# One block of the first MLP product moved across a chunk boundary on TensorE, and two bias sums held back in the tail

## What is computed

```
n  = layernorm(x)                                   # no gain or bias
h  = layernorm(n) * ln1_g + ln1_b
q, k, v = h@wq, h@wk, h@wv                           # 16 heads of 16
phi = elu(.) + 1
num = phi(q) @ (sum over the sequence of phi(k)^T v)
den = phi(q) . (sum over the sequence of phi(k))
y2 = n + (num / den) @ wo                            # 256 x 256
g  = layernorm(y2) * ln2_g + ln2_b
t  = gelu at the grid point nearest to g@w1          # steps of 0.1, w1 256 x 1024
xp = x + (y2 + t @ w2)                               # w2 1024 x 256
out = xp + (layernorm(xp) @ CB^T) * SCB/127 + bias   # CB 256 x 256
```

## Time and profile before

| what | value |
| --- | --- |
| median of 3 runs | 593.51 us |
| the profiled execution | 594.68 us, its span 592.9 us |
| mean granted TensorE clock | 0.981 of full speed |
| TensorE matrix multiplications | 549.6 us busy, 93% |
| VectorE | 466.2 us, 79% |
| ScalarE | 384.8 us, 65% |
| GpSimd | 338.8 us, 57% |

### The profile page before, as it was taken

The page is one execution under the profiler, slowest core; times in us unless marked ns, Lnnn a source line. Parts: engine busy times, 40 slices in busy tenths (PEclk is TensorE's granted clock), DMA queues, the critical chain, the costliest instruction groups (busy, mean ns, idle before and its releaser), DMA issues.

```text
span 592.9 us, 11272 instructions
## 1 busy us (share of the span) xinstructions
PE 549.6 (93%) x3610; PEld 490.9 (83%) x3610; DVE 466.2 (79%) x1067; ACT 384.8 (65%) x636; POOL 338.8 (57%) x328
## 2 busy tenths in 40 slices
PE   6899999999996889999999999999999999999893
PEld 6778788888885879889898898988988889898783
DVE  5889998688775487978879788788887888878645
ACT  2475664465565667858669586696865968758650
POOL 3431333324131367786776868768687676776662
PEclk9699998999999999999999999999999999999998
DMA  8321221121001010101101101011010110200001
GB/s 269 122 71 48 94 71 37 35 72 35 16 22 56 1 37 1 71 35 35 71 0 71 39 33 71 0 71 54 16 71 0 71 68 2 71 4 33 36 21 54
DMA packets 11419, 29.47 MB, mean 50 GB/s; under 512 B 2048, under 2 KB 4864, under 8 KB 11392
## 3 DMA queue, kind: packets, MB, share of 16 engines
q1 hardware_dynamic: 9472, 28.32, 13.4%
q10 hardware_dynamic: 1920, 0.79, 0.7%
HBM read 20.71 MB, written 8.39 MB: 49 GB/s over the span
## 4 chain that ended last, share of the span: by engine, by line
DVE 28%; PE 23%; issue 18%; ACT 15%; POOL 13%; DMA 2%; POOLq 1%; ACTq 0%; DVEq 0%; SPq 0%
PE psum L1002 22%; POOL f32r_arena L378 7%; DVE bn_stats L657 4%; ACT grid_index L580 3%; POOL f_arena L371 3%; DVE f_arena L793 3%; DVE f32r_arena L814 3%; ACT f32r_arena L593 3%; DVE f_arena L824 2%; DMA f_arena<-in_L_attn_x_dram 2%; DVE f32r_arena L810 2%; DVE bn_stats_b L657 2%; ACT f_arena L591 2%; ACT f32r_arena L528 2%; DVE f32r_arena L802 2%
## 5 line engine op out<-in xcount | busy, mean ns | idle before, releaser
L1002 PE MATMUL psum<-w_hi,f32r_arena 128*128 128x256 f32 x1280 | 176.9, 284 | 12.3 <-POOL f32r_arena L378 8.6
L1002 PEld LDWEIGHTS psum<-w_hi,f32r_arena 128*128 128x128 f32 x1280 | 164.0, 189 | 22.9 <-issue 16.9
L1002 PE MATMUL psum<-f32r_arena,w_hi 128*128 128x512 f32 x512 | 139.9, 403 | 1.5 <-issue 1.0
L378 POOL TENSOR_TENSOR f32r_arena<-f_arena,f32r_arena 128x512 fp32r<-128x512 f32 x64 | 85.9, 1342 | 94.6 <-ACT f32r_arena L593 54.1
L580 ACT ACTIVATE grid_index<-psum,w_bias_in_steps 128x512 int8<-128x512 f32 x128 | 86.7, 677 | 64.2 <-PE psum L1002 64.2
L1002 PEld LDWEIGHTS psum<-f32r_arena,w_hi 128*128 128x128 f32 x512 | 88.0, 188 | 19.9 <-ACT grid_index L580 5.8
L591 ACT ACTIVATE f_arena<-grid_index 128x512 f32<-128x512 int8 x128 | 80.9, 632 | 24.6 <-POOL f32r_arena L378 14.3
L593 ACT ACTIVATE f32r_arena<-grid_index 128x512 fp32r<-128x512 int8 x128 | 79.3, 619 | 0.0
L1002 PE MATMUL psum<-f32r_arena 128*128 128x256 f32 (+1 forms) x384 | 71.6, 336 | 2.0 <-DVE f32r_arena L696 2.0
L1002 PEld LDWEIGHTS psum<-f32r_arena 128*128 128x128 f32 x384 | 59.2, 195 | 8.4 <-issue 2.2
L802 DVE TENSOR_TENSOR f32r_arena<-f_arena,f32r_arena 128x512 fp32r<-128x512 f32 x64 | 63.2, 988 | 2.1 <-ACT f32r_arena L593 1.8
(11 more groups left out here) (116 smaller groups left out, 916.2 us busy)
## 6 DMA issues: line engine op xcount, KB each, us to landing
f_arena<-in_L_attn_x_dram SPq DMA_DIRECT2D x32, 512.0 KB, 3.3
out_dram<-f_arena SPq DMA_DIRECT2D x15, 512.0 KB, 2.7
f_arena<-in_L_attn_w_dram SPq DMA_DIRECT2D x2, 1024.0 KB, 12.6
out_dram<-f_arena SPq DMA_DIRECT2D x2, 256.0 KB, 3.3
phi_q<-in_L_attn_wk_dram ACTq DMA_DIRECT2D x1, 256.0 KB, 4.7
phi_q<-in_L_attn_wq_dram SPq DMA_DIRECT2D x1, 256.0 KB, 4.9
phi_q<-in_L_ffn_CB_dram SPq DMA_DIRECT2D x1, 256.0 KB, 7.0
phi_q<-in_L_attn_wo_dram SPq DMA_DIRECT2D x1, 256.0 KB, 7.5
```

Of the source, the lines that this page charges most:

```text
L378: nc.gpsimd.tensor_tensor(t_lo[m % SLOTS], tf[m % 2], t_hi[m % SLOTS].bitcast(F32), ALU.subtract).then_inc(s["t_lo_p"], 1)
L1002: return nc.tensor.matmul(out_, lhs, rhs, start=start, stop=stop, skip_group_check=True)
```

## The change

TensorE takes `up(i + 1, 0)` before `down(i, 7)` instead of behind it; the very first `up(0, 0)` stays where it was. GpSimd waits, ahead of its two sums in the tail, until both halves are normalised. No operation is added or taken away, apart from that wait. A line that is only "..." marks what is left out.

```diff
@@ the tail of GpSimd's program
             g.wait_ge(stored, CHUNKS * 16)
+            g.wait_ge(s["n_half"], 2)
             for h in range(2):
                 nc.gpsimd.tensor_tensor(half_tm(xb, h).rearrange("p (j d) -> p j d", j=TT // 2),
...
@@ TensorE, phase 2
                 def body(i, prv, main, nxt, attend_seq, attended):
                     if main:
-                        up(i, 0)
                         up(i, 1)
...
                     down(i, 6)
                     if attend_seq is not None:
                         attention(i + 2, attend_seq, 1)
+                    if nxt:
+                        up(i + 1, 0)
                     down(i, 7)
 
+                up(0, 0)
                 body(0, False, True, True, 0, 0)
```

## The result

The changed kernel takes 595.1 us (median of 12 runs) where the one before takes 592.8 in the same sessions: a ratio of 1.004, interval 1.002 to 1.0059, so about 2.4 us slower. I had predicted 1.2 us slower, inside a range of 591.0 to 598.4. The profiled execution has a span of 593.6 us, 0.7 us longer than that of before.

The account below looks back on a forecast made before the run. It took each chunk as bound by VectorE's chain from `down` 7 to `attention_out` plus TensorE's stretch after it. Boundaries + 3.5 and tail - 2.3 made + 1.2 us on 593.5, so 594.7 us, range 591.0 to 598.4.

Parts of the forecast that it names:

- The joint: `down` 7 at a chunk boundary: from it to `attention_out` the time is VectorE's, 7.09 us; the rest is TensorE's.
- the slack: Free time ahead of `down` 7, counted between starts: 0.71 us, where the moved block needs 0.94 us.
- The size at the boundaries: Cost of the moved block at 13 chunk boundaries: + 3.5 us in all, bounded by 0 and + 7.7 us.
- the bracket: Listed wait of TensorE ahead of `down` 7, counted from the modelled end of the last multiplication: 0.46 us.
- the 0.23 us of the working: At a chunk boundary `down` 7 ends this much later, and the delay passes on to `attention_out`.
- The rule on the sustained stream: About 131 ns per 512-column multiplication, so the moved block takes 0.52 us and fits; the forecast used 235 ns instead.
- the rival that hung on it: The block is hidden in the wait ahead of `down` 7 and boundaries cost 0: 591.2 us, faster; chance 0.12.
- The last chunk: The boundary behind chunk 14, with 1.3 us of listed wait, was to cost nothing.
- The tail: Second half normalised in 0.71 us instead of 2.62, GpSimd's sums held back: - 2.3 us, bounds - 1.8 and - 2.7.
- The sums cover: GpSimd's held-back bias sums finish before line 996 needs them, with 0.4 us to spare for the second.
- The lower bound of the boundaries: Boundaries cost at least 0: a loop of `down` 7, VectorE and GpSimd's four `mlp_low` already takes the whole period.
- The wait ahead of `down` 0: TensorE reaches `down` 0 sooner and stands there for VectorE, some 0.7 to 0.9 us on line 802.

Follow-up runs that it names:

- half block: Against the changed kernel, only the first 2 of `up` 0's 4 multiplications stand ahead of `down` 7, the other 2 behind it: 589.3 us, 0.9929 of before.

## Why the prediction held, and where it didn't

- **The joint.** Right. `down` 7 to `attention_out` belongs to VectorE, and what stands ahead of `down` 7 is paid once the slack is used up. The body's length against the number of multiplications in front: 0 gives 24.44 us, 2 give 24.35, 3 give 24.50, 4 give 24.75, 8 give 25.6 while the clock holds. From 4 to 8 it is 0.22 us each, near the 0.235 from the starts of two blocks.
- **The size at the boundaries.** + 3.5 us forecast, + 3.8 - 0.1 us measured. The slack was read rightly from starts and not from the bracket, within 0.1 us. At the boundary shown, `up` 1 starts 2.80 us after the half of `attention` (338.15 - 335.35), where without the move `up` 0 started 2.57 us after it (335.49 - 332.92): the 0.23 us of the working. Two slips in the working change nothing. The sum of the brackets is 5.5 us and not 5.4, and 334 to 335.49 is 1.5 us and not 1.6. And `down` 7 has no wait for GpSimd at 13 boundaries and not at 14: 0.17 us are left behind chunk 0, and 0.37 behind chunk 14.
- **The rule on the sustained stream** (the Trainium skill, "TensorE: Matmul & The Clock Gate", section "Back-to-back issue gap") gave 0.52 us for the block, and then no loss. The block takes 337.21 - 336.19 = 1.02 us here. The trace disagrees with the Trainium skill for this data type and this mix, and the rival that hung on it fell.
- **The last chunk.** This is the step that failed: "behind chunk 14 ... have more slack than 0.94 and cost nothing". The boundary itself cost nothing, as written. The chunk behind it lost 0.8 us, since the block's early end moved VectorE's subtractions onto the start of GpSimd's power (+ 0.3 us) and of its `mlp_low` 2 (+ 0.5 us). I had looked at what ScalarE's lead would give back and not at what it would collide with. This is most of the distance between + 1.2 and + 2.4 us. That the time itself, 595.1, is only 0.4 us from the 594.7 forecast is in part luck: the kernel before took 592.8 us in these sessions and not the 593.5 that I had added to.
- **The tail.** - 2.3 us forecast, - 2.5 us in the stretch and - 2.1 us in the medians. Each step of the working is in the rows. The sums cover as foreseen: nothing waits for them.
- **The lower bound of the boundaries.** I argued that they can't gain, because a loop through GpSimd already takes the whole period. The half block has bodies of 24.35 us, so the loop isn't closed as I drew it. ScalarE starts on `up` 0 1.64 us after the start of `down` 7 there and 2.15 us before the change; whether that is the way by which 0.1 us is gained was not tested and stays open.
- **The wait ahead of `down` 0** was forecast at 0.7 to 0.9 us, and is 0.77 or 0.85 by turns.

## What to carry to other kernels

Where the work behind an idle gap is the start of another engine's chain, the gap can be filled without loss only up to its slack, measured between starts. Cut the filler to the size of the gap: with the same wait in the tail, half of this block made 0.9929 of the time before, none of it 0.9959, and all of it 1.004. The step from all to half is clear of the noise, that from none to half is not. And ask of every step that becomes early which engine it now shares a moment with, and which of the two starts first.

## What the runs showed of the hardware

- Behind a wait of about 1.7 us TensorE's granted clock fell to 0.50 for some 3 us in 8 of 13 bodies, though the engine was busy again by then, and each fall cost 1.6 us. In the other 5 the same wait was followed by none. Behind waits of 0.85 us in the same place of the changed kernel there was none. In chunk 0, with two waits of 1.4 and 2.4 us, it fell in 6 of 13 profiles of kernels that are the same up to there; from the start of `down` 0 to the first sum of `xp` the fall costs 1.5 us (27.0 against 25.4 or 25.5 us), and that much of the scatter of single runs can be this.
- The Trainium skill, "TensorE: Matmul & The Clock Gate", section "What's actually happening", has these two levels, 1.2 and 2.4 GHz. The two products in the tail show the ratio only in part, 3.45 us at the lower level against 2.33 at the higher.
- Of two subtractions with both inputs in SBUF, one on VectorE and one on GpSimd, the one that started later took longer. `mlp_low` 2 on GpSimd took 1.80 us where VectorE's `mlp_low` 3 had started 0.02 us ahead of it, and 1.27 us where it started 0.35 us first; there `mlp_low` 3 took 1.47 us instead of 0.69. GpSimd's power took 1.34 us where it started into a subtraction; where the subtraction started 0.22 us behind it, neither took longer (1.02 and 0.69 us).
- A `tensor_scalar` of VectorE with one input took 1.3 us for 256 columns beside GpSimd's sums and 0.36 us alone, while an instruction with one operand in PSUM was not touched by the same sums.
